# Attention between two mixture-of-experts layers: the router's second logits taken from eight extra columns, and the work of both attention passes put in another order

## The reference

```
x = x + 0.5 * ffn(layernorm(x))      # router of 8 experts, the top 2 of each token, gate/up 256x512, down 256x256
x = x + attn(layernorm(x))           # 16 heads of 16, rotary, no softmax
x = x + 0.5 * ffn(layernorm(x))      # same weights as the first
attn: q, k, v = x@Wq+bq, x@Wk+bk, x@Wv+bv ; q, k = rope(q), rope(k)
      ctx = (q k^T / 4) v per head ; ctx@Wo + bo
ffn:  logits = x @ router_weight (256x8); softmax over the top 2
```

## Time and profile before

| | us |
|---|---|
| median of 3 runs | 738.54 |
| the profiled execution | 740.95 |
| its span in the profile | 739.1 |

### The profile page before, as it was taken

How to read it: one execution, slowest core, us unless ns; L and a number is a source line. 1 busy time by engine, 2 the same in 40 slices (tenths; PEclk the granted TensorE clock), 3 DMA queues, 4 the chain that set the end, 5 groups by cost and what they waited for, 6 DMA issues and landing times.

```text
span 739.1 us, 13830 instructions
## 1 busy us (share of the span) xinstructions
PE 609.8 (83%) x3900; PEld 538.8 (73%) x3901; DVE 455.2 (62%) x1130; ACT 360.4 (49%) x800; POOL 411.9 (56%) x444
## 2 busy tenths in 40 slices
PE   3782489999999999788997799459999999999700
PEld 3781378888888888767776799448888888888600
DVE  4557946555555555388885588684555555555356
ACT  4884424545455554378875244233454555554300
POOL 2445555777777774369996100007577777776400
PEclk9999999999999999999999899659999999999955
DMA  9675032322333331434431442113222333222189
GB/s 324 226 212 168 1 117 77 92 98 92 98 98 98 99 92 52 142 117 140 158 101 58 142 158 100 57 1 91 77 92 94 98 99 98 93 95 78 50 313 369
DMA packets 52018, 88.01 MB, mean 119 GB/s; under 512 B 15634, under 2 KB 31425, under 8 KB 51468
## 3 DMA queue, kind: packets, MB, share of 16 engines
q1 hardware_dynamic: 21334, 43.69, 17.9%
q0 software_dynamic: 13664, 35.42, 15.3%
q10 hardware_dynamic: 16982, 8.43, 3.9%
HBM read 53.96 MB, written 35.39 MB: 121 GB/s over the span
## 4 chain that ended last, share of the span: by engine, by line
PE 62%; DVE 12%; DMA 9%; POOL 7%; ACT 5%; issue 4%; SPq 1%; ACTq 0%; DVEq 0%; POOLq 0%
PE ps L820 15%; PE ps L822 15%; PE ps L821 15%; PE ps L811 10%; DMA work<-y_dram 4%; PE ps L815 3%; POOL aT_lo L523 2%; PE ps L838 2%; DMA xn_dram<-work 2%; DVE xs L1349 1%; DVE work L1263 1%; POOL xn_lo L517 1%; ACT work L566 1%; POOL work L513 1%; POOL work L514 1%
## 5 line engine op out<-in xcount | busy, mean ns | idle before, releaser
L484 POOL DMA_INDIRECT y_dram<-work,sidx x142 | 143.1, 1008 | 73.5 <-issue 42.2
L476 POOL DMA_INDIRECT work<-xn_dram,gidx x142 | 145.9, 1028 | 46.6 <-issue 42.5
L811 PE MATMUL ps<-cst,work 128*128 128x128 f32 x824 | 133.4, 288 | 26.9 <-ACT work L566 21.5
L811 PEld LDWEIGHTS ps<-cst,work 128*128 128x128 f32 x824 | 104.7, 150 | 40.4 <-issue 14.0
L820 PE MATMUL ps<-up_hi,xT_hi 128*128 x284 | 118.1, 416 | 1.0 <-DVE xT_lo L1293 1.0
L822 PE MATMUL ps<-up_hi,xT_lo 128*128 x284 | 112.1, 395 | 0.0
L821 PE MATMUL ps<-up_lo,xT_hi 128*128 x284 | 111.9, 394 | 0.0
L670 ACT ACTIVATE work<-ps 128x256 f32<-128x256 f32 x142 | 54.7, 385 | 108.0 <-PE ps L822 108.0
L1308 DVE TENSOR_SCALAR work<-ps 128x256 f32<-128x256 f32 x142 | 59.8, 421 | 65.6 <-ACT work L670 65.0
L679 ACT ACTIVATE work<-ps,slot_gate 128x256 f32<-128x256 f32 x142 | 59.8, 472 | 81.2 <-PE ps L822 81.2
L1290 DVE SCALAR_TENSOR_TENSOR slot_gate<-work,sign,second 128x1 f32<-128x1 f32 x142 | 25.5, 219 | 101.5 <-ACT xT_hi L656 101.5
(11 more groups left out here) (157 smaller groups left out, 1406.1 us busy)
## 6 DMA issues: line engine op xcount, KB each, us to landing
work<-y_dram SPq DMA_DIRECT2D x32, 512.0 KB, 5.0
xs<-L_attn_x SPq DMA_DIRECT2D x4, 1024.0 KB, 10.0
work<-L_ffn_gate_up_proj SPq DMA_DIRECT2D x8, 512.0 KB
q_dram<-work ACTq DMA_DIRECT2D x16, 256.0 KB, 2.7
work<-q_dram SPq DMA_DIRECT2D x16, 256.0 KB, 2.7
out<-xs SPq DMA_DIRECT2D x16, 256.0 KB, 5.9
xn_dram<-work SPq DMA_DIRECT2D x16, 255.0 KB, 3.7
xn_dram<-work ACTq DMA_DIRECT2D x16, 255.0 KB, 2.2
```

The lines of the kernel that those rows point to most:

```text
L476: pool.indirect_dma_start(xg[:, k, u, 1:H + 1], None, xn_dram[n], bass.IndirectOffsetOnAxis(ap=gidx[:, 2 * s + u:2 * s + u + 1], axis=0)). ...
L484: pool.indirect_dma_start(y_dram[n], bass.IndirectOffsetOnAxis(ap=sidx[:, 2 * s + u:2 * s + u + 1], axis=0), ysb[:, k, u, :], None, bounds ...
L811: ins = nc.tensor.transpose(ps[:, bank, k:k + P], src[:, u, c * P:(c + 1) * P], ident)
```

## The change

In words:
- The second layer's logits are no longer computed from transposed normalised rows. In the first pass, PE makes 8 more matmuls of 16 columns per group (`router`, in bank 7) with the x it already has, and DVE folds them (`router_out`). M gets 8 more columns (NB = 264), made in the middle, so that `attend` gives the attention's share of the logits too, and `add_out` adds it with a second small add. The gap of the two best logits is then scaled by `inv_all`.
- First pass, order. `a_in(g)` stands between the two halves of `project(g-1)`; `xT_high(g)` between the two copies of `qk_out(g-1)`. `scale_and_shift(g+1)` and `normalise(g+1)` are made in step g, at its end, ahead of `k_high(g-2)` and `store_q(g-2)`.
- Second pass. ACT normalises in place of DVE; the transposes, `xn_out`, `logits` and `logits_out` go. DVE has `scale_and_shift` in place of `inverse` and `normalise`.
- Middle. Wo is transposed on PE, ACT copies it, and small products give the 8 columns and the logits' constant; DVE scales the logits once.
- Key sums use one PSUM bank in place of two. A load of bo as a column (256 pieces of 4 bytes) is added to SP's list behind Wo's.

The core of the diff:

```diff
@@ scalar, first_pass
             def first_pass(g, j, it):
                 b, static = j % 2, isinstance(g, int)
-                if not (static and g >= NG):
-                    wait(act, xn_lo, g - 3)
-                    normalise(A, xn_a[:, j], g, b, first=1)
                 if not (static and g < 2):
                     xn_high(g - 2, (j + 2) % 4)
                     scale_cos(g - 2, b)
+                def high():
+                    if not (static and g >= NG):
+                        xT_high(g, b)
                 if not (static and not 1 <= g <= NG):
-                    qk_out(g - 1, 1 - b, it * 2 + (j - 1) // 2)
-                if not (static and g >= NG):
-                    xT_high(g, b)
+                    qk_out(g - 1, 1 - b, it * 2 + (j - 1) // 2, high)
+                else:
+                    high()
                 if not (static and g >= NG - 1):
                     sqrt_var(A, 1 - b, g + 1)
+                    wait(act, xn_lo, g - 2)
+                    normalise(A, xn_a[:, (j + 1) % 4], g + 1, 1 - b, first=1)
                 if not (static and g < 2):
                     k_high(g - 2, b)
                     store_q(g - 2, b)
...
-            for g in range(NG, NG + 2):
-                first_pass(g, g % 4, g // 4)
+            first_pass(NG, NG % 4, NG // 4)
+            act.wait_ge(mid_pe, 1)
+            nc.scalar.activation(woT, ps[:, 0, :].rearrange("p (c v) -> p c v", c=KC), ACT.Copy).then_inc(mid_act, 1)
+            first_pass(NG + 1, (NG + 1) % 4, (NG + 1) // 4)
@@ scalar, second_pass
+                wait(act, L[1].xn_stored[j], 16 * it)
+                normalise(L[1], xn_r[j], g, b)
                 if not (static and g + 3 >= NG):
                     q_high(g + 3, 1 - b)
-                norm_step(L[1], 1, g, b, first=static and g == 0)
+                act.wait_ge(L[1].xn, g + 1)
+                act.dma_start(pair(xn_v[1], g)[:, :, 0:H - 1], xn_r[j][:, :, 1:H]).then_inc(L[1].xn_stored[j], 16)
+                if not (static and g == NG - 1):
+                    sqrt_var(L[1], 1 - b, g + 1)
@@ tensor, project
-            def project(g, b):
+            def project(g, b, between=None):
                 for u in range(2):
+                    if u == 1 and between is not None:
+                        between()
...
+                wait(pe, pre_done, g)
+                for u in range(2):
+                    router = ps[:, 7, u * 2 * E:(u + 1) * 2 * E]
+                    for c in range(KC):
+                        nc.tensor.matmul(router, xT[0][:, b, u, c, :], wr_parts[:, c, :], start=c == 0, stop=False)
+                        ins = nc.tensor.matmul(router, xT[1][:, b, u, c, :], wr_parts[:, c, :], start=False,
+                                               stop=c == KC - 1)
+                ins.then_inc(pre_ps, 1)
@@ tensor, second_pass
-                xn_transpose(l, g, b)
-                if not (static and g < 1):
-                    logits(l, g - 1, 1 - b)
             stages(pe, second_pass)
-            logits(l, NG - 1, 1)
@@ vector, first_pass
-                scale_and_shift(A, g, b)
                 def turn():
                     if not (static and g < 2):
+                        router_out(g - 2)
                         rotate(g - 2, b)
...
                 xT_low(g, b)
+                if not (static and g == NG - 1):
+                    scale_and_shift(A, g + 1, 1 - b)
+
+            def router_out(g):
+                dve.wait_ge(pre_ps, g + 1)
+                parts = ps[:, 7, 0:4 * E].rearrange("p (u k e) -> p u e k", u=2, k=2)
+                v.tensor_reduce(pair(logit, g), parts, AX.X, ALU.add).then_inc(pre_done, 1)
@@ vector, second pass
-                v.tensor_tensor(xr, xr, ps[:, 4 + b, :].rearrange("p (u h) -> p u h", u=2), ALU.add).then_inc(x_done, 1)
+                v.tensor_tensor(xr, xr, ps[:, 4 + 2 * b:6 + 2 * b, 0:H], ALU.add)
+                v.tensor_tensor(pair(logit, g), pair(logit, g), ps[:, 4 + 2 * b:6 + 2 * b, H:NB],
+                                ALU.add).then_inc(x_done, 1)
...
-                inverted = inverse(l1, g, b)
+                scale_and_shift(l1, g, b)
                 if not (static and g + 1 >= NG):
                     add_out(g + 1, 1 - b)
-                wait(dve, l1.xn_stored[b], 16 * k)
-                normalise(l1, xn_r[:, b], g, b, inverted)
```

More of the change, by code:

```diff
@@ L51 @@
 NCONST = C_E + E
-NB = H
+NB = H + E
 Q32, Q64 = 32, 64
@@ L234, in build @@
         wv = area(6784, KC, H)
[L235 removed]
+        wo = area(7296, KC, H + E)
+        share = area(7824, P)
+        bo_col = area(7952, KC)
+        no_weights = area(7956, P, dt=BF16)
+        woT = area(0, KC, H)
+        bo_wide = area(1028, KC, P)
         gT = area(516, KC, H)
         sT = area(1284, KC, P)
[L240 to L242 removed]
+        first_hot, second_hot = [area(at, NT, E, dt=BF16) for at in (2576, 2704)]
+        both_hot = area(2832, NT, E, dt=BF16)
+        ahead = area(2960, NT + 2, E, dt=BF16)
         equal, candidate = [area(at, NT, E) for at in (1536, 1792)]
[L244 removed]
+        running = area(1024, 2, PAD + NT, E, dt=BF16)
         top = area(7040, 2, NT)
@@ L583, in logits_out, with norm_step @@
                                      ACT.Copy).then_inc(l.logit_sb, 1)
[L585 to L588, removed]
+            def norm_step(l, g, b, first=False):
+                xn_out(l, g, b)
                 if not first:
@@ L721, in xT_high, with qk_out @@
                                      ACT.Copy).then_inc(A.x_hi, 1)
-            def qk_out(g, b, k):
+            def qk_out(g, b, k, between):
                 wait(act, q_stored[b], 16 * k)
@@ L985, in project, with clear_sums, key_sums @@
                     ins.then_inc(qk_ps, 1)
-            def key_sums(g, b, first=False, last=False):
+                wait(pe, pre_done, g)
[6 more added lines that the diff above has]
+                ins.then_inc(pre_ps, 1)
+            def clear_sums():
+                for c in range(KC):
+                    nc.tensor.matmul(ps[:, 6, c * H:(c + 1) * H], no_weights, biases[:, 0:H], start=True, stop=False,
+                                     skip_group_check=True)
+            def key_sums(g, b, last=False):
                 pe.wait_ge(xn_lo, g + 1)
@@ L1001, in first_pass, with turn @@
                 static = isinstance(g, int)
-                if not (static and not 1 <= g <= NG):
-                    project(g - 1, (j + 1) % 2)
-                if not (static and g >= NG):
-                    a_in(g, j)
-                if static and g == 0:
-                    keep_running(12)
+                def turn():
+                    if not (static and g >= NG):
+                        a_in(g, j)
+                    if static and g == 0:
+                        keep_running(12)
+                if not (static and not 1 <= g <= NG):
+                    project(g - 1, (j + 1) % 2, turn)
+                else:
+                    turn()
                 if not (static and g < 3):
-                    key_sums(g - 3, (j + 1) % 2, first=static and g == 3, last=static and g == NG + 2)
+                    if static and g == 3:
+                        clear_sums()
+                    key_sums(g - 3, (j + 1) % 2, last=static and g == NG + 2)
             keep_running(80)
@@ L1216, in route @@
                 v.engine_nop().then_inc(l.mask, 1)
-                v.tensor_tensor(small[:, 16:16 + NT], top[:, 1, :], top[:, 0, :], ALU.subtract).then_inc(l.gap, 1)
+                gap = small[:, 16:16 + NT]
+                ins = v.tensor_tensor(gap, top[:, 1, :], top[:, 0, :], ALU.subtract)
+                if n == 1:
+                    st.done(ins)
+                    ins = v.tensor_tensor(gap, gap, inv_all[:, :], ALU.mult)
+                ins.then_inc(l.gap, 1)
                 for stored in l.xn_stored:
@@ L1415, in _ @@
             moments(A, 0, 0)
+            scale_and_shift(A, 0, 0)
+            dve.wait_ge(qk_lo, 1)
+            v.memset(share, 1.0 / H)
+            v.memset(no_weights, 0.0)
             st.stages(12, first_pass)
-            for g in (NG - 2, NG - 1):
-                rotate_whole(g, g % 2)
-                key_low(g, g % 2)
-            dve.wait_ge(out_w_loaded, 64)
-            fold_rows(wv, first_row[:, 1, 0:H])
+            router_out(NG - 2)
+            rotate_whole(NG - 2, 0)
+            router_out(NG - 1)
+            dve.wait_ge(out_w_loaded, 80)
+            v.tensor_copy(bo_wide, bo_col[:, :, None].to_broadcast([P, KC, P]))
+            key_low(NG - 2, 0)
+            dve.wait_ge(mid_pe, 1)
+            v.tensor_tensor(wr_mid[:, :, :], wr_fold[:, :, :], ps[:, 1, None, 0:E].to_broadcast([P, KC, E]),
+                            ALU.subtract).then_inc(mid_dve, 1)
+            rotate_whole(NG - 1, 1)
+            key_low(NG - 1, 1)
+            fold_rows(wv, first_row[:, 1, 0:H])
+            dve.wait_ge(mid_pe, 2)
+            v.tensor_copy(wo[:, :, H:NB], ps[:, 1, E:3 * E].rearrange("p (a e) -> p a e", a=KC))
```

(3 more changed lines are left out.)

142 lines of the change are left out of this document (88 added, 54 removed).

## The result

The changed kernel takes 742.84 us (median of 20 runs, 740.52 to 745.99); the kernel before took 738.92 beside it (20 runs, 735.58 to 742.01). The ratio is 1.0054, with a 95% interval of 1.0042 to 1.0067: 3.9 us slower. The forecast was 744.5, slower.

What follows compares the result with a forecast made beforehand. POOL was taken to bound the first pass, PE the second. The terms 10.6 - 0.6 + 2.6 + 0.8 - 7.4 gave +6.0 us: 746.95 on the profiled execution, 744.5 against the median; range 734 to 754.

Steps and rivals of the forecast that it cites:

- What bounded the kernel, and which step decides: First pass: POOL bounds it; k_high falls behind normalise, so k_lo and the next qk_out come later, a period of 6.35 us against 5.47.
- s: First pass: the time at which ACT starts qk_out(g-1), from which the forecast counts the step's other times.
- The price of k_lo: First pass, POOL: two instructions, 1.45 us, or 1.89 when an add of DVE falls beside them; 1.9 taken.
- The store of q: First pass: issued right after k_high starts, at s + 3.75, landing 2.7 us later at s + 6.45; the next qk_out waits for it.
- Twelve steps at +0.88: First pass: twelve steps each 0.88 us longer, +10.6 us in all.
- The last step: First pass: the last of 13 steps has no normalise ahead of k_high, so it takes 4.9 us: -0.6.
- The turned halves of project gain nothing: First pass, PE: they shorten PE's wait for x_lo, but PE isn't what is late, so no gain.
- The walk from group 2's adds: Start of the first pass: step 3's qk_out at 328.6 where it was 326.00, +2.6 us (bounds +1 and +4).
- the load of bo: Start: bo's column, issued on SP ahead of group 2's load, takes about 0.4 to 0.5 us.
- The middle: Between the passes: ACT waits for PE's transposes of Wo and copies them before the last group's cosines: +0.8 us (bounds 0 and +2).
- Second pass: DVE becomes the bound in place of PE, with a step of 3.01 us against 3.36: -7.4 us (bounds -4.5 and -10.5).
- The rival of a falling clock: Second pass: PE's clock falls as PE idles, half the steps at 4.4 us, +11 us, 755; chance 0.06.

Runs made afterwards that it cites:

- e5: Kernel before, with only scale_and_shift(g+1) and normalise(g+1) moved to the end of step g, ahead of k_high(g-2) and the store of q: 751.60 us, ratio 1.0180.
- e2: Changed kernel with 2 of the 8 small router matmuls per group (second layer's logits incomplete): 741.38 us, ratio 1.0041.
- e4: Changed kernel with only the store of q moved ahead of normalise(g+1), k_high staying behind: 743.64 us, ratio 1.0055.
- e9: Changed kernel with a_in(g) put back behind both halves of project(g-1), nothing else: 747.31 us, ratio 1.0101.
- e1: Changed kernel with k_high(g-2) and the store of q put back ahead of normalise(g+1) in the first pass: 744.89 us, ratio 1.0081.
- e13: Changed kernel without the small add of add_out in the second pass (second layer's logits lack the attention's share): ratio 1.0009, on a slower chip.

## Why the prediction was right

**What bounded the kernel, and which step decides: right, shown.** `qk_out` waits for `k_lo`, and moving the normalise ahead of `k_high` makes that late. The forecast put `k_high` at s + 3.62 and the next `qk_out` at s + 6.3; the trace has 349.04 - 345.46 = 3.58 and 6.25. e5 makes the loss with this one step, e2 and e4 rule out PE and the store.

**The price of k_lo.** It was taken at 1.9, from the earlier trace rows, because an add of DVE falls beside it. The changed kernel has 1.88 with the add beside it, e5, whose add is over 0.1 us after `k_lo` starts, 1.42. The Trainium skill's page "SBUF — State Buffer", section "Who interferes with whom", says that a DVE instruction with two SBUF inputs contends with a GpSimd instruction that reads SBUF; both traces agree. In e5 the cheaper `k_lo` didn't help, since `xT_high` comes 0.5 later there.

**The store of q: wrong, without effect.** It was reckoned to be issued after `k_high` starts, to land at s + 6.45. The trace has the issue at s + 2.94 (348.40), ahead of `k_high` itself, while the normalise of 348.04 still runs on the engine; it lands 2.2 us later (2.1 to 2.8), at s + 5.1. That is why the step came out at 6.25, POOL's path alone, and not at 6.35.

**Twelve steps at +0.88: direction right, size off.** They took 400.31 - 326.78 = 73.5, or 6.13 each, +0.66 and +7.9 in all. The steady ones are 6.25; the last three take 5.7 to 5.9, and the walk didn't treat them apart. In the first two of these, DVE's second add starts 0.4 ahead of `k_lo` and not beside it, and `k_lo` takes 1.61 instead of 1.88. The last step took 4.64 where 4.9 was forecast.

**"The turned halves of project gain nothing": right in the steady part, wrong at the start.** The walk from group 2's adds gave 328.6 for step 3's `qk_out`. The changed kernel has 326.78; e9, which lacks the turn, 328.89. So at the start the turn is on the path, by `xT_high`, which waits for the transposes in e9 and not in the changed kernel; the walk gave it no gain there either. That e9 lies near the walk's 328.6 is chance: its adds of group 2 came at 313.85, 1.2 us earlier. A smaller part of the error of 1.8 us is the load of bo, which was to hold these adds back by 0.4 to 0.5: they start at 315.04 in the changed kernel, 315.03 before. The forecast also missed the turn's other effect, that it ties normalise to the key sums (e1).

**The middle: +2.6, not +0.8; half of it is the change's.** The forecast looked at ACT's wait for the transposes of Wo. The copy of Wo does put off the last cosines, by 0.7. A term is missing beside it: ACT's timeline shows `k_high(14)` waiting 1.79 us for key sums, which the router matmuls push back, and everything of the last group stands behind it. It starts 2.89 after the last `qk_out`, 2.08 in the kernel before, and 2.17 in e2, which has 2 router matmuls:

```profile
404.95 1.10 ACT L752 ACTIVATE work<-ps 128x512 f32<-128x512 f32 x2 [0.59 <-DMA q_dram<-work]
407.84 0.63 ACT L774 ACTIVATE aT_hi<-work 128x512 fp32r<-128x512 f32 x1 [1.79 <-PE ps L1045]
...
408.56 0.60 ACT L803 ACTIVATE work<-ps 128x512 f32<-128x512 f32 x1
```

The rest is the clock. The timeline of PE and DVE has the last key sums:

```profile
413.65 0.55 PE L1043 MATMUL ps<-aT_hi,xn_hi 128*128 128x256 f32 x1 [1.40 <-DVE aT_lo L1466]
...
416.59 0.69 DVE L1528 COPY work<-ps 128x512 f32<-128x512 f32 x1 [1.49 <-PE ps L1045]
```

PEclk is 0.50 there (the stretch 413 to 417): 12 matmuls start 0.21 apart, where those of the group before start 0.12 apart, 1.1 us more. The changed middle isn't what decides it: e5, with the middle as before, has its last key sums at half clock too, and e13, with the changed middle, has them at full clock. What does decide it stays open. One matmul of each, from PE's timelines of e5 and e13:

```profile
416.96 0.41 PE L997 MATMUL ps<-aT_hi,xn_lo 128*128 128x256 f32 x1
...
457.75 0.28 PE L1045 MATMUL ps<-aT_hi,xn_lo 128*128 128x256 f32 x1
```

From the last `qk_out` to the copy of the key sums e13 takes 10.40 us (448.75 to 459.15, on another chip), the kernel before 9.03: some 1.4 is what the changed middle costs where the clock holds.

**Second pass: -8.9, not -7.4.** DVE is the bound, as forecast (e13). Its 15 steps from 429.99 to 473.93 take 2.93 each, against 3.01: the ones written out take 2.8, those in the loop 2.9 to 3.3, the longest with an idle 0.34 marked "issue" ahead of line 1547. The step's 0.08 is 1.2 of the 1.5 us. The rival of a falling clock is refuted: PEclk is 1.00.

**Routing: -1.5, not foreseen.** Some 1.1 of it is that the filler matmuls ahead of the experts ran at the full clock in the changed kernel: 50 of them took 5.62 us, and 7.29 before. This is the clock of one execution and not an effect of the change: e5, whose routing is that of the kernel before, has 5.62 too, and e2, whose routing is the changed one, 7.02 (PE's timelines of e5 and e2).

```profile
510.68 5.62 PE L877 MATMUL ps<-cst 128*128 128x128 f32 x50
...
498.23 7.02 PE L909 MATMUL ps<-cst 128*128 128x128 f32 x50
```

**The sum.** Up to routing the traces have +1.8 where the walk had +6.0: 1.8 less at the start, 2.9 less in the first pass and 1.5 more saved in the second, against 2.1 lost around the middle. The medians differ by 3.9. Some 2 us of that no stage of the two traces shows; it is the 2.0 by which the profiled execution of before lies above its median, and isn't resolved by stage. So the direction and the step that decides it were reasoned out, but that 744.5 lies within 1.7 us of 742.84 is partly luck: four terms were off by 1.5 to 2.9 us each, in both directions, and the last 2 us up to the medians are unexplained.

## What to carry to other kernels

Where an instruction is moved ahead of another on the same engine, follow the one that falls behind to whoever waits for it: `k_high` sat in a gap in which ACT waited anyway, and moving it out of the gap cost more than the new order could bring. When removing a cause makes the kernel slower, as in e1, look for a second loop of nearly the same length, and remove both: the one alone cost 2 us, the other alone brought 1 to 1.5 (within the noise), together they brought 8. Before a difference between two traces is put down to a change, look at the clock of the same stretch in the other variants: here it came and went with the execution, 1.1 us at a time. Within an engine's queue, work for which nobody waits soon (the router matmuls) goes behind the work on whose end a buffer hangs (the key sums); that and `k_high` in its gap turn this change from 0.5% slower to 0.3 to 0.6% faster.

## What the runs showed of the hardware beyond the forecast

With weights of its own, a matmul of few columns costs here what one of 256 does. In the changed kernel the 16-column router matmuls start 0.11 us apart (but for the first two of a group, 0.02), the 256-column key sums 0.12. PE's timeline, two starts of each:

```profile
345.08 0.26 PE L1025 MATMUL ps<-wr_parts,xT_lo 128*128 128x16 f32 x1
...
345.19 0.26 PE L1024 MATMUL ps<-wr_parts,xT_hi 128*128 128x16 f32 x1
...
346.68 0.28 PE L1045 MATMUL ps<-aT_hi,xn_lo 128*128 128x256 f32 x1
...
346.80 0.28 PE L1043 MATMUL ps<-aT_hi,xn_hi 128*128 128x256 f32 x1
```

The Trainium skill's page "TensorE: Matmul & The Clock Gate", section "LDWEIGHTS (loading the stationary operand)", gives about P / 1.2 ns for P columns of weights. An estimate from it for the 128 here is 107 ns, and the 0.11 measured agrees with the reading that each of these matmuls pays for loading its own 128 columns of x; no run here varies the number of weight columns.
